# A language-model tower on one core: the token stage in another order, and the first projection cut into halves between its tiles

## What is computed

```python
h = where(is_hot, hot_emb_w[tok2hot], cold_emb_w[tok2cold] @ proj_w.T)   # [2, 1024, 512], latent 128
h = h + attention(layernorm(h), w_project, w_out)                        # causal, 16 heads of 32
h = h + moe(layernorm(h), Wr, bias, Wg, Wu, Wd, sWg, sWu, sWd)           # 16 experts, top 2, and a shared one
```

## Time and profile before

| | us |
|---|---|
| median of 3 runs | 1100.26 (1097.65 to 1100.49) |
| the profiled execution | 1100.8 |
| its span, first to last instruction | 1099.0 |
| PE busy in the span | 982.8 (89%) |
| DVE, ACT, POOL busy | 558.8, 485.2, 299.6 |
| first scores of unit 0 | at 128.42 |

### The profile page before, as it was taken

One profiled execution on the slowest core, in us unless ns is written; L12 is line 12 of the kernel. 1 busy time (PEld: TensorE's weight loads), 2 busy tenths in 40 slices (PEclk: granted clock), 3 DMA queues, 4 the chain that ended last, 5 costly groups with the idle time before them and its releaser, 6 DMA issues.

```text
span 1099.0 us, 21945 instructions
## 1 busy us (share of the span) xinstructions
PE 982.8 (89%) x6623; PEld 647.5 (59%) x6624; DVE 558.8 (51%) x1645; ACT 485.2 (44%) x1163; POOL 299.6 (27%) x319
## 2 busy tenths in 40 slices
PE   7668599999989999899988899899998999899994
PEld 5224458586766858577676687678543444344441
DVE  8875267575746657466677677578311111111110
ACT  7122277776747677676778422211121222122221
POOL 1376120201102020110102046333133443344442
PEclk9689799999989999999999999999999999999998
DMA  5134534331513334150533111611397457855453
GB/s 203 40 101 108 133 78 107 78 78 43 114 33 78 79 78 97 37 129 4 122 112 117 68 68 58 268 42 46 104 286 195 85 94 231 247 95 86 86 93 41
DMA packets 44575, 114.38 MB, mean 104 GB/s; under 512 B 9332, under 2 KB 11380, under 8 KB 42162
## 3 DMA queue, kind: packets, MB, share of 16 engines
q1 hardware_dynamic: 32146, 87.14, 27.1%
q0 software_dynamic: 12320, 25.90, 12.5%
HBM read 53.03 MB, written 25.17 MB: 71 GB/s over the span
## 4 chain that ended last, share of the span: by engine, by line
PE 64%; issue 11%; DMA 9%; DVE 7%; POOL 4%; ACT 3%; DVEq 0%; POOLq 0%; ACTq 0%
PE psum L1243 10%; PE psum L511 9%; DMA out<-y_sb,slot_out 8%; PE psum L481 7%; PE psum L501 6%; PE psum L524 6%; PE psum L486 5%; PE psum L1322 5%; PE psum L1187 4%; PE psum L1171 3%; PE psum L1264 2%; PE psum L1286 1%; PE psum L527 1%; DMA x_rows<-xn_scratch,slot_tok 1%; POOL hot_all L1410 1%
## 5 line engine op out<-in xcount | busy, mean ns | idle before, releaser
L636 DVE CUSTOM_DVE_ANT_0 psum<-psum,mask_row 128x128 f32<-128x128 f32 (+7 forms) x256 | 195.3, 766 | 77.8 <-PE psum L501 57.3
L593 ACT ACTIVATE probs<-psum,nmax 128x128 f32<-128x128 f32 (+7 forms) x256 | 190.2, 743 | 78.7 <-DVE nmax L636 68.7
L1243 PE MATMUL psum<-attnT,x_T 128*128 x376 | 181.4, 605 | 5.6 <-issue 3.9
L501 PE MATMUL psum<-k_stack,q_stack 128*128 128x512 f32 (+2 forms) x384 | 154.2, 457 | 31.3 <-issue 16.5
L511 PE MATMUL psum<-ident,probs 128*128 128x128 f32 x1152 | 174.8, 277 | 5.4 <-ACT probsT L578 3.1
L511 PEld LDWEIGHTS psum<-ident,probs 128*128 128x128 f32 x1152 | 137.9, 142 | 35.9 <-issue 15.1
L1144 DVE COPY x_T<-psum 128x512 f32<-128x512 f32 x47 | 32.5, 692 | 242.8 <-PE psum L1286 242.8
L578 ACT COPY probsT<-psum 128x512 f32<-128x512 f32 (+3 forms) x256 | 128.8, 503 | 37.4 <-PE psum L511 29.6
L481 PE MATMUL psum<-xnT,w_unit 128*128 128x512 f32 x256 | 132.3, 606 | 0.2 <-ACT full L456 0.2
L428 POOL CAST part_hi<-full 128x512 fp32r<-128x512 f32 x32 | 19.6, 613 | 371.7 <-ACT full L456 264.9
L844 POOL DMA_INDIRECT out<-y_sb,slot_out x47 | 74.5, 1586 | 169.0 <-DMA out<-y_sb,slot_out 93.9
(11 more groups left out here) (216 smaller groups left out, 1394.0 us busy)
## 6 DMA issues: line engine op xcount, KB each, us to landing
attnT<-in_wgu SPq DMA_DIRECT2D x16, 1024.0 KB, 5.3
q_stack<-part_hi SPq DMA_DIRECT2D x64, 128.0 KB, 2.4
q_stack<-part_lo SPq DMA_DIRECT2D x64, 128.0 KB, 2.4
k_stack<-part_hi SPq DMA_DIRECT2D x64, 128.0 KB, 2.4
k_stack<-part_lo SPq DMA_DIRECT2D x64, 128.0 KB, 2.6
w_dn<-in_wd SPq DMA_DIRECT2D x16, 512.0 KB, 6.2
out<-acc SPq DMA_DIRECT2D x17, 256.0 KB, 3.8
hot_all<-xn SPq DMA_DIRECT2D x4, 1024.0 KB, 8.4
```

What stands on the lines that cost most here:

```text
L501: mm = pe.matmul(dst[:, c0:c1], qs, k_stack[b][:, h, c0:c1], start=True, stop=True)
L593: act.activation(probs[n % PSLOTS][:, 0:(i + 1) * P], bank(2 * (n % 2), 2)[:, 0:(i + 1) * P], ACT.Exp, bias=nmax[:, n % 4:n % 4 + 1], scal ...
L636: dve.tensor_tensor_reduce(out=row, in0=row, in1=mask_row[:, (QT - 1 - i) * P:QT * P], scale=1.0, scalar=3.0e38, op0=ALU.add, op1=ALU.min, ...
L1243: mm = pe.matmul(bank(2 + p), lhs(k), rhs(k), start=(k == 0), stop=(k == KC - 1), skip_group_check=True)
```

## The change

Six things are changed, all ahead of the first scores.

1. Twelve look-ups stand ahead of the tiles (EARLY_LOOKS) instead of sixteen. The last four stand in the token loop, in steps 1 to 4, with their row numbers behind DVE's step 4. Since banks 1 and 5 are in use by then, odd ones go to bank 7.
2. LAG is 1, so POOL has the inverse deviation of tile c - 2 behind the gathers of tile c.
3. The pieces of unit 0 stand in steps 7, 8, 9, 11, 12 and 13 (FIRST_FILL): q, k and v of the first 512 tokens, then q, k and v of the second. A piece waits for four or eight tiles of `xnT`.
4. ACT takes the high part and DVE the low part of these pieces straight out of PSUM (`first_high`, `first_low`). `full` and POOL's `split_part` are not used for unit 0. A piece waits for the low part of the piece before it.
5. The q stack is still issued by SP, behind the store of tile 12. The k stack is issued by ACT, in its step 14.
6. `stack_room`, a placeholder in SBUF, stands elsewhere, and SP, ACT and DVE wait for all 16 stores to `h_scratch` before they go into attention.

```diff
-LAG = 4
+LAG = 1
+EARLY_LOOKS = 12
+FIRST_FILL = {7: 0, 8: 2, 9: 4, 11: 1, 12: 3, 13: 5}
-FILL0 = NT // BATCH + 3
...
-                sp.wait_ge(s_lo, HEAD + 4 * u + 2 * side + 2)
+                sp.wait_ge(s_lo, HEAD + (3 + side if first else 4 * u + 2 * side + 2))
...
+        def look_bank(c):
+            return bank(4 if c % 2 == 0 else 5 if c < EARLY_LOOKS else 7)
...
+        def first_high(act, c):
...
+            act.wait_ge(s_fill, HEAD + n + 1)
+            if side == 0:
+                act.activation(part_hi[:, 0, cols], bank(7), ACT.Copy, scale=-ATT_SCALE).then_inc(s_hi, 1)
+            elif side == 1:
+                act.copy(part_hi[:, 1, cols], bank(7)).then_inc(s_hi, 1)
+            elif half == 0:
+                act.copy(v_unit[0][:, 0:4, :].rearrange("p a n -> p (a n)"), bank(7)).then_inc(s_fact, 1)
...
+        def first_low(dve, c):
...
+            if side < 2:
+                dve.wait_ge(s_hi, HEAD + 2 * half + side + 1)
+                if side == 0:
+                    dve.scalar_tensor_tensor(out=part_lo[:, 0, cols], in0=bank(7), scalar=-ATT_SCALE,
+                                             in1=part_hi[:, 0, cols].bitcast(F32), op0=ALU.mult,
+                                             op1=ALU.subtract).then_inc(s_lo, 1)
+                else:
+                    dve.tensor_tensor(part_lo[:, 1, cols], bank(7), part_hi[:, 1, cols].bitcast(F32),
+                                      ALU.subtract).then_inc(s_lo, 1)
+            elif half == 1:
+                dve.wait_ge(s_fill, HEAD + n + 1)
+                dve.tensor_copy(v_unit[0][:, 4:8, :].rearrange("p a n -> p (a n)"), bank(7)).then_inc(s_fdve, 1)
...
+        def first_piece(pe, c):
+
+            f = FIRST_FILL[c]
+            pe.wait_ge(s_w, 16)
+            pe.wait_ge(s_xC, 4 * (f % 2) + 4)
+            if f == 0:
+                pe.wait_ge(s_looked, 2 * NT)
+            elif f == 1:
+                pe.wait_ge(s_fact, HEAD + 3)
+            else:
+                pe.wait_ge(s_lo, HEAD + {2: 1, 4: 2, 3: 3, 5: 4}[f])
+            for k in range(KC):
+                fill_products(pe, 0, f, k)
...
-                if c == NT - LAG:
+                if c == NT - 4:
                     stack(sp, 0, 0, (0,), first=True)
-            stack(sp, 0, 0, (1,), first=True)
+            sp.wait_ge(s_hst, 16 * NT)
...
-                if c < NT - 1:
-
-                    half = c - NT + LAG + 1
-                    split_part(pool, 0, 0, half // 2, half % 2, None)
...
-                if 0 <= c - FILL0 < FILLS:
-                    fill_evac(act, "act", 0, c - FILL0, 0)
+                if c in FIRST_FILL:
+                    first_high(act, c)
+                if c == 14:
+                    stack(act, 0, 0, (1,), first=True)
+            act.wait_ge(s_hst, 16 * NT)
...
             for c in range(NT + 1):
+                if c - 1 in FIRST_FILL:
+                    first_low(dve, c - 1)
                 if c < NT:
                     embed(c)
                 if c >= 1:
                     norm(c - 1)
-                if 0 <= c + 1 - FILL0 < FILLS:
-                    fill_evac(dve, "dve", 0, c + 1 - FILL0, 0)
+                if 1 <= c <= NT - EARLY_LOOKS:
+                    look_up(EARLY_LOOKS + c - 1)
+                if c == NT - EARLY_LOOKS:
+                    row_numbers(BATCHES - 1)
+            dve.wait_ge(s_hst, 16 * NT)
...
-                if 0 <= c - FILL0 < FILLS:
-
-                    pe.wait_ge(s_xC, NT // BATCH)
-                    for k in range(KC):
-                        fill_piece(pe, 0, 0, c - FILL0, k, 16)
+                if 1 <= c <= NT - EARLY_LOOKS:
+                    look(EARLY_LOOKS + c - 1)
+                if c in FIRST_FILL:
+                    first_piece(pe, c)
```

More of the change, by code:

```diff
@@ L1367, in _ @@
         def _(pool):
-            for s in (s_lo, s_hi):
-                pool.sem_inc(s, HEAD)
             pool.memset(xn[:, 0, :], 0.0).then_inc(s_zeros, 1)
@@ L1427, in _ @@
         def _(act):
-            for s in (s_E, s_Ca, s_fact, s_ZR):
+            for s in (s_E, s_Ca, s_fact, s_ZR, s_hi):
                 act.sem_inc(s, HEAD)
+            act.sem_inc(s_fact, 2)
             act.wait_ge(s_const, 9)
@@ L1459, in _ @@
         def _(dve):
-            for s in (s_M, s_Cd, s_Zr, s_Z, s_AT, s_fdve):
+            for s in (s_M, s_Cd, s_Zr, s_Z, s_AT, s_fdve, s_lo):
                 dve.sem_inc(s, HEAD)
+            dve.sem_inc(s_fdve, 2)
             step = Chain(dve, s_dve)
@@ L1552, in norm @@
                                   ALU.subtract, ALU.mult).then_inc(s_xn, 1)
-            for k in range(BATCHES):
+            for k in range(EARLY_LOOKS // PER):
                 for c in range(k * PER, (k + 1) * PER):
@@ L1591, in _, with look @@
             pe.wait_ge(s_tohC, 2)
-            for c in range(NT):
+            def look(c):
                 if c >= 2:
                     pe.wait_ge(s_looked, 2 * (c - 1))
-                b = bank(4 + c % 2)
+                b = look_bank(c)
                 oh = tok_ohT[:, c, :]
@@ L1600, in _ @@
                           skip_group_check=True).then_inc(s_look, 1)
+            for c in range(EARLY_LOOKS):
+                look(c)
             pe.wait_ge(s_proj, 16)
```

16 lines of the change are left out of this document (13 added, 3 removed).

## The result

| | before | after |
|---|---|---|
| median of the runs | 1100.38 us (1097.65 to 1101.65, 4 runs) | 1121.20 us (1118.48 to 1122.57, 4 runs) |
| profiled execution, time / span | 1100.8 / 1099.0 us | 1121.23 / 1119.5 us |
| granted clock, mean | 0.967 | 0.955 |
| first scores of attention | 128.42 us | 145.48 us |

The ratio is 1.019, with a 95% interval of 1.0163 to 1.0217. The prediction said 1110.4 us, in a range of 1103 to 1116: slower was right, but the loss is 21 us and not 10, and it lies outside the range.

A forecast was written before the change was run, and what follows sets the result against it. Attention was taken to start when the k stack lands, at 128.42 us; the steps moved first scores to 138.5, so 1100.8 + 10.1 = 1110.9 us, 1110.4 by the median, range 1103 to 1116.

The forecast's parts named there:

- Step 1: Start of the tiles: with twelve look-ups ahead, first sum on DVE at 53.2, not 58.75: 5.5 us earlier.
- Step 2: First sum to first piece: adds 3.6 us for late look-ups, 1.7 for LAG 1, 0.7 for half clock; piece at 76.5.
- Step 3: Six pieces: each waits for the previous low part, 7.7 us a turn, 38.7 together; last piece starts at 115.2.
- rival D: Token stage: more of it at 1.2 GHz, a piece taking 7.2 us; 1114.0 or 1117.6 us; chance 0.07.
- Step 4: k stack on ACT: 16 copies start at 120.9 and take 10.2 us; ACT free at 131.1.
- rival B: Stacks: q and k contend, ACT free up to 4 us later, 1114.5 us; chance 0.10.
- Rival A: Stack on ACT: DMAs handed off at next to nothing, 1101.6 us, or 1097.1 with the clock kept; chance 0.12.
- Step 5: Behind ACT's copies: the last tile's chain waits, 7.3 us partly at 1.2 GHz; first scores at 138.5.
- Step 6: The rest: waits for the h stores just covered, attention's start costs the same; 10.1 us slower in sum.
- signs of being wrong: Wrong if ACT copies beside its DMAs, pieces stand 5 us apart, or the time changes behind the first scores.

The follow-up runs named there:

- e10: Kernel after with LAG = 2 instead of 1 and nothing else: median 1114.19 us, ratio to before 1.0118 to 1.0156.
- e1: Kernel after with the k stack issued by SP behind all the stores and nothing issued by ACT: median 1119.39 us.
- e4: Kernel after with the q stack behind SP's store of tile 11 instead of tile 12: median 1118.95 us.
- e7: Kernel before with its k stack issued by ACT in step 16, plus the three waits for the stores: median 1100.38 us.
- e11: Kernel before with only the change's three waits for all 16 stores added: median 1100.93 us, ratio 0.9988 to 1.0016.
- e5: Kernel after with low parts as in e2 and both stacks on SP behind the store of tile 10: median 1102.20 us.
- e2: Kernel after with each low part on DVE behind the norm of its own piece's tile: median 1104.51 us.
- e9: e6 with LAG = 2 and the k stack behind the store of tile 12: median 1094.13 us, ratio to before 0.9933 to 0.9966.
- e6: e5 with the second halves of q, k and v at steps 10 to 12 and the stacks behind the store of tile 9: median 1100.79 us.
- e12: Kernel after with the edits of e2 and e10 together, stacks still on two queues: median 1099.17 us.
- e3: Kernel after with LAG = 4 instead of 1: median 1122.14 us, ratio to before 1.0193 to 1.0227.
- e8: Kernel after with all 16 look-ups ahead of the loop instead of 12: median 1126.75 us.

## Why the prediction was wrong, by its steps

**Step 1** held: first sum at 53.2 predicted, 52.85 measured.

**Step 2** gave the right number by errors that cancel. First piece at 76.5 predicted, 75.39 measured (75.39 to 78.82 over six kernels). Three terms were off. The pace of before was read too slow: tile 1 is turned 2.3 us behind tile 0, not 3.14, and tile 4 at 75.14, 16.4 us behind the first sum and not 17.3:

```profile
75.14 0.66 PE L1626 MATMUL psum<-ident,xn 128*128 128x128 f32 x4 [1.51 <-DVE xn L1551]
```

The look-ups had been given 3.6 us, and the half clock 0.7. In e10, which has the look-ups in the loop but not the loop of LAG = 1, tile 4 is turned at 70.66, 17.8 us behind the first sum, so that both together cost 1.4. A look-up takes DVE 0.8 us, and in before DVE waits 0.81 for POOL in every tile. I credited that gap once; each look-up fills that of its own tile (sums 2.99, 3.05 and 3.11 us apart in e10, and no wait of DVE), and only the row numbers come on top (the next sum 4.46 behind). And LAG = 1 had been given 1.7, for one late gather of tile 3, whose tile 2 came as predicted (sum at 60.16, 60.3 predicted). But it costs 4.2 against e10, up to 7.7 in the other executions, and is paid in the tiles behind too. I followed the first late gather and did not ask whether the wait closes a loop.

**Step 3** is the first step that failed, in size. The mechanism is right: every piece waits for the low part of the one before, behind the sum of the next tile, and where the clock is full the turn is 7.65 to 7.73 us (e1), for 7.7 predicted. But the five distances of after make 44.15 us (75.39 to 119.54), not 38.7. The sum took a piece at 3.6 us in a turn in which it had itself just made TensorE stand (2.65 us as measured). Three pieces took 5.4 us, which is 5.0 of the 5.4 us that are missing. This is rival D in kind, though not in place: it looked at the thin stretch ahead of the pieces, gave a whole piece at 7.2 us and held one or two of them for 0.07 likely. The trace of before had the warning, a clock of 0.51 at 66 to 68 us after a thin stretch. So the step that failed is the price of a piece: 3.6 us taken, 5.4 measured behind three of four stands. Last piece at 119.54 instead of 115.2: 4.3 us.

**Step 4** failed in size too, by what rival B held possible. ACT starts at 124.80 (3.9 later than the 120.9 predicted, the delay of step 3) and issues for 13.5 us, not 10.2. The value on an undisturbed queue, 10.6 in e4, is well met; the rest goes when the q stack is out of the way (e4). q's start was predicted at 113.4 and came at 117.58, so the overlap was near what I had computed, 3.6 us for 2.7, but its price was put at a chance of 0.10 instead of into the sum. That two engines issue at once is not the whole reason (e4), and what is was not found out. Rival A is out by this row, by e7 and by e1.

**Step 5** held: from ACT free to first scores 7.1 us (138.38 to 145.48), 7.4 predicted, with the projection at 2.08 us as in the step.

**Step 6** held for the waits: they cost nothing in after, nor in e11. But after is 20.4 us longer in the profiled execution and only 17.1 of it are there at the first scores. That the time changes behind the first scores was one of my signs of being wrong, and it did, by 3.4 us. The granted clock shows with what they go. Added up from windows of half a microsecond, TensorE is at 1.2 GHz for 38.2 us behind the first mask operation in before's execution, for 48.5 in after's and for 48.5 in e11's, whose program is before's there and which took 973.4 us for this stretch where after took 973.25. Over all fourteen it is 38.2 (969.8 us) to 55.4 (e5, 976.9 us), by and large in order, with exceptions (e10 49.4 and 970.8). So the 3.4 us need no work that the change would have added: the execution of before had the fullest clock of the fourteen, and e11's shows as much without the change. Why the clock fell there in one execution and not in the other is not shown. Nor is whether a small part of the loss in the medians lies behind the first scores: the median less the first mask operation of the profiled execution is 975.0 us for after, 971.2 for before and 970.2 to 975.9 for the twelve kernels.

The account for the first scores: 138.5 + 4.3 (pieces; less 0.4 on the way to ACT's first copy) + 3.3 (ACT's longer issues) - 0.3 (tail) = 145.4, measured 145.48. The range had room for either error, 4 us for B or 3.6 for one slow piece, not for both (1110.4 + 7.0 = 1117.4) and the 3.4 behind the first scores. Both errors come from taking durations out of a stretch in which nothing disturbed them. One reading is off without touching the sum: rival A counts 9 us at half clock behind the first scores of before, and the windows there are at full clock again from 136.2, so 7.8.

What was hoped of the change did not come true for reasons that e2, e10 and e9 separate: the low parts in the wrong place in DVE's row (14.05 us at the first scores), LAG too small by one (4.55), and the stacks' place and queue (6.9 from the first piece on, between e2 and e5; of the queue alone, 2.1 in e1, which two executions can also differ by). Without these, and with the second halves a step earlier, which e6 alone doesn't show to help, the kernel is 5.4 us faster than before (e9).

## What to carry over

When an operation waits for the next step of another engine's row, ask what that step needs in turn: twice here (low part behind the next sum, gather behind the inverse deviation) the answer was an instruction of the engine that waits, and the loop set the pace. Take a duration from a stretch that idles as the new one will; a matmul priced after a full stretch is too cheap after a stand. A depth such as LAG can lose at both ends: 1 closes a loop, 4 puts the gathers of six tiles ahead of the first result, and a trial of one of them says nothing about 2. And before a difference of a few microseconds is put down to an edit, look at a stretch in which the two programs are the same: here it differed by up to 3.4 us ahead of the first piece and by more behind the first scores.

## What the runs showed of the hardware

- Issuing a copy of 128 KB from SBUF to SBUF occupies ACT as it does SP: a median of 0.62 us on ACT in e4, 0.59 on SP, and no instruction of ACT behind it starts until it is through (11.4 us in e7, 13.0 in after). The Trainium skill, "DMA: Bandwidth & Descriptors", section "Issuing engines are not separate DMA queues", calls what a second issuer saves usually small. The runs agree: the first scores come at 126.57 with the k stack on ACT (e7) and at 126.61 with it on SP (e11).
- A single issue can take much longer: up to 1.93 us on ACT in after, 1.7 us behind SP's last one of the other stack, and up to 2.19 us on SP alone in before. 16 copies on ACT took 10.6 us (e4) to 14.6 us (e12).
- A stand of only 2.65 us between two busy stretches can be followed by 1.2 GHz for part of the next piece: 5.12 to 5.44 us instead of 3.60 to 3.81 in 19 of 24 pieces behind one (after, e1, e3, e4, e8, e10). Not each stand is: in e1 the first two pieces behind one ran in 3.67 and 3.81, in after the last. What decides it, no run here tells.
- Behind the first scores, where the instructions are the same, TensorE was at 1.2 GHz for 38 to 55 us in the fourteen profiled executions, and the stretch took 970 to 977 us.
